# Graph and mixture-of-experts layer: another order of TensorE's work in the mixing part, ranks by a running sum, routing in three steps

## The chip, the cores and the metric

The kernel runs on one core of a Trainium2 chip. The time is the device time of one execution in microseconds (us), the median of three runs. Its engines are TensorE (PE in the profile; PEld are its weight loads), VectorE (DVE), ScalarE (ACT), GpSimd (POOL) and SyncE (SP), which here only issues DMAs.

## What is computed

6250 tokens of 256 numbers, fp32 in and out. Cut to what matters:

```python
xn = layernorm(x)
x = x + graph(xn, src, dst) + mixing(xn)      # mixing: linear attention; it comes down to xn @ M + b
f = layernorm(x)
rh = relu(f @ router_w1 + router_b1)          # 256 -> 128
p = softmax(rh @ router_w2 + router_b2)       # 128 -> 6 experts
top_w, top_i = top_k(p, 2); w = softmax(top_w)
x = x + sum_k w[k] * expert[top_i[k]](f)      # three layers of 256x256, relu after the first two
```

## The kernel before

The program has four stages: tokens are normalised and turned, and the graph's rows are made; keys, values and their products, with the gathers of the graph beside them; the mixing part (some 280 to 440 us of the span); the expert part (to the end). The change is in the third.

**Tokens.** Token `p * 50 + t` stands in partition p (125 of them) and tile t (50). Two tiles are a pair, and the mixing part goes over 25 pairs. Pairs are put together in groups (`SIZES`, six groups of 4, 5, 5, 4, 4, 3 pairs), and routing is done once for each group. A group's rows stand in one of four buffers `xr` until they are scattered.

**One pair.** TensorE makes `x_h @ mix_h + x_h @ mix_l + x_l @ mix_h` and the bias (`mix`, lines 1240 to 1250, 14 products). VectorE adds the token and the graph's sum, and takes mean and variance (`mixed_rows`, L987, L991, L994). ScalarE takes the root (L697); VectorE makes 1/root and -mean/root (`finish2`, L1002, L1004), and the next pair's sum of token and graph (`graph_rows`, L967). ScalarE normalises (L705), TensorE turns the tiles (`turn_rows`, L1259), ScalarE copies them from PSUM (L708), TensorE multiplies by the router's first layer (`hidden`, L1268), ScalarE does the relu (L693), and TensorE the router's second layer (`logits`, L1283; for a group's first pair it starts with the bias, L1279).

**The steps.** Each engine's program is a loop over `i` that is written out by hand, in which pair i is mixed while older pairs are at later stations. TensorE's step i: `hidden(i-2)`, `ranks` of a group whose last pair is i-5, `mix(i+1)`, `logits(i-2)`, `turn_rows(i-1)`. ScalarE's step: relu of i-2, root of i, normalising and eviction of i-1, then an exponential of the routing where one is due. Root and exponential need different function tables, and each change of table is an instruction of its own (ACT_TABLE_LOAD). VectorE's step: `mixed_rows(i)`, `finish2(i-1)`, `graph_rows(i+1)`, then parts of the routing.

**The routing of a group** has four parts on VectorE (`route`, lines 1006 to 1053), in four different steps: part 0 (step of last pair + 2) takes the maximum of the logits; part 1 (+3) the softmax and the first choice of expert; part 2 (+4) the second choice; part 3 (+5) the weights, and the row number of every token in the table of its expert. The one-hot choices are `oh`. The row numbers come from `ranks` on TensorE: one product with a triangle `tri` for the partitions above, one with `base`, the rows already given away, and one more for every tile but the last, which counts it into all later ones. They stand between the second choice and part 3. After part 3 GpSimd scatters the group's tiles into the table `tab0` in DRAM, one indirect DMA for each tile (L566), 50 in all.

**The end of the part.** When all groups are through, one product gives the experts' row ends (L1314), and VectorE makes the tables for the expert part on one partition: how many tiles of 128 rows each expert has (a comparison of 16 x 49 numbers, L1085, L1086), their running sum (L1088, L1090), and for each of 54 tiles and both choices the first row and the expert (L1093 to L1105). SyncE writes six blocks of rows that are to be skipped behind the experts' rows (L453), waits for the tables and all scatters, and loads the first tiles (L469). TensorE, ScalarE and VectorE wait for `tab_done` of both choices before the expert part.

Of the kernel before, what the change touches and what calls it, by code (L numbers as in the profile page):

```python
# [20 lines left out]
P = 125  # L21
# [13 lines left out]
SIZES = (4, 5, 5, 4, 4, 3)  # L35
# [22 lines left out]
AL_STEPS, R_STEPS = 6, 20  # L58
ROUTE_STEPS = (0, 1, 9, 14)
# [3 lines left out]
POOL_C = 14  # L63
# [10 lines left out]
def gps_layer(nc, x, src, dst, w_kv, w_q, w_oT, b_out, w_g, a_l, a_r, rw1, rb1, rw2, rb2,  # L74
              ew1, eb1, ew2, eb2, ew3, eb3, out):
    ctx = ExitStack()
    with ctx:
# [103 lines left out]
        oh = sb("oh", [P, Q, 2, EP], FP32R)  # L181
        rk = sb("rk", [P, Q, 2, EP])
        tw = sb("tw", [P, 8, Q])
        posf = sb("posf", [P, Q, 2])
        pos0 = sb("pos0", [P, RB, Q], I32)
        base = sb("base", [P, 2, EP])
        bsum = sb("bsum", [P, 2, EP])
# [3 lines left out]
        NM = -(-N // S)  # L191
        cnt = sb("cnt", [1, 2, EP])
        nmul = sb("nmul", [1, NM])
        ntl = sb("ntl", [1, 2, EP])
        ge_at = 2 * EP * NM
        gn_at = ge_at + 2 * NTT * E
        tf_at = gn_at + 2 * NTT * E
        ncmp = gsum_sb[0:1, 0:ge_at].rearrange("p (k e m) -> p k e m", k=2, e=EP)
        ends = sb("ends", [1, 2, EP])
        jj = sb("jj", [1, NTT])  # L200
        ge = gsum_sb[0:1, ge_at:gn_at].rearrange("p (k j e) -> p k j e", k=2, j=NTT)
        gn = gsum_sb[0:1, gn_at:tf_at].rearrange("p (k j e) -> p k j e", k=2, j=NTT)
        tf = gsum_sb[0:1, tf_at:tf_at + 16 * NTT].rearrange("p (s k j) -> p s k j", s=8, k=2)
# [44 lines left out]
        rk_ps = d_ps[0:P, 0:Q * 2 * EP].rearrange("p (g k e) -> p g k e", g=Q, k=2)  # L248
# [39 lines left out]
        cnt_done, tstep, tab_done, fill_out = sem("cnt_done"), sem("tstep"), sem("tab_done"), [sem(f"fill_out{k}") for k in range(2)]  # L288
# [196 lines left out]
        def _(pool):  # L485
# [47 lines left out]
            for t in range(T):  # L533
                m, b = t // CH, t // CH % 2
                if t % CH == 0 and m >= 2:
# [14 lines left out]
                      allow_small_or_imprecise_dtypes=True).then_inc(pool_c, 1)  # L550
            pool.iota(desc[:, :], pattern=[[-1, EP]], base=EP, channel_multiplier=0,
                      allow_small_or_imprecise_dtypes=True).then_inc(pool_c, 1)
            pool.iota(tok_all[:, :], pattern=[[1, T]], base=0, channel_multiplier=T).then_inc(pool_c, 1)
            pool.iota(nmul[:, :], pattern=[[S, NM]], base=0, channel_multiplier=0,
# [50 lines left out]
        def _(act):  # L605
# [83 lines left out]

            def step(i):  # L690
                if 0 <= i - 2 < PR:
                    act.wait_ge(rh_done, i - 1)
                    act.activation(rhT[:, :], rh_ps[:, 0:2 * P], ACT.Relu, bias=rb1_sb[:, 0:1]).then_inc(rhT_done, 1)  # L693
                if i < PR:
                    part = slice(i % 2 * 2, i % 2 * 2 + 2)
                    act.wait_ge(ag2_done, 2 * i + 2)
                    act.activation(sd[:, part], mv[:, part, 1], ACT.Sqrt, bias=eps_sb[0:P, 0:1]).then_inc(sd2_done, 1)  # L697
# [22 lines left out]
            for i in range(PR + 6):  # L720
                step(i)
# [678 lines left out]
```

## Time and profile before

| what | us |
| --- | --- |
| median of 3 runs | 796.24 (793.36 to 800.51) |
| the profiled execution's own time | 797.89 |
| its span | 795.7 |
| busy: PE, DVE, ACT, POOL | 676.3, 559.5, 443.0, 402.5 |
| mean granted clock of TensorE | 0.944 of 2.4 GHz |

The span is the time from the first to the last instruction of the profile; the execution's own time has 2.2 us around it. Busy time counts each engine's own instructions; a wait is the idle time before one. In rows of the timeline the columns are start, duration, engine, line, operation, written and read tiles, shape, how many, and in brackets the idle time before it with what ended it. One name can cover several uses: in the mixing part `kv_ps` holds the mixed rows, the hidden layer and some logits, `pt` the turned tiles, `staged` the normalised and the turned rows.

### The profile page before, as it was taken

Reading aid. Unit: us, or ns where it says so; the run is one execution under the profiler, and the core shown is the slowest. Engines: PE = TensorE matmul, PEld = TensorE weight load, DVE = VectorE, ACT = ScalarE, POOL = GpSimd, SP = SyncE. Lnnn points to the kernel's source line nnn. Section 1 sums busy time; section 2 is a strip of 40 time slices with the busy share of each in tenths; the row PEclk is TensorE's granted clock in tenths of the full one; section 3 lists DMA queues with packets and bytes.
Section 4 is the critical chain, followed back from the end, with each engine's and each line's share of the span. In section 5 each row is a group of like instructions: output and inputs, shape, how many; then the busy total and the mean of one; then the engine's idle time right before and its main releaser. Section 6 shows DMA issues by size and latency. Waiting matters only on the chain.

```text
span 795.7 us, 15452 instructions
## 1 busy us (share of the span) xinstructions
PE 676.3 (85%) x4744; PEld 622.7 (78%) x4744; DVE 559.5 (70%) x1399; ACT 443.0 (56%) x874; POOL 402.5 (51%) x443
## 2 busy tenths in 40 slices
PE   3878999999999888888850799999994899999992
PEld 2767788888888777777640699999994799999992
DVE  5674679888888757777645477777773477777772
ACT  2545566767777436677630555656651566565640
POOL 3455378876666000454536155555555155465553
PEclk9999999999999999999955799999998799999997
DMA  8885644444443445765324523443432535444420
GB/s 215 190 157 121 159 125 135 143 127 120 139 125 98 149 145 168 227 187 165 105 59 119 172 89 125 141 137 129 133 115 95 158 92 145 130 134 140 125 74 29
DMA packets 72463, 106.24 MB, mean 134 GB/s; under 512 B 24612, under 2 KB 45605, under 8 KB 72386
## 3 DMA queue, kind: packets, MB, share of 16 engines
q1 hardware_dynamic: 51074, 72.57, 32.4%
q0 software_dynamic: 21312, 32.69, 13.4%
q8 instruction: 43, 0.70, 0.4%
q14 instruction: 34, 0.28, 0.1%
HBM read 60.32 MB, written 46.78 MB: 135 GB/s over the span
## 4 chain that ended last, share of the span: by engine, by line
PE 76%; ACT 6%; DMA 5%; DVE 4%; issue 3%; POOL 3%; SPq 1%; POOLq 0%; DVEq 0%; ACTq 0%
PE kv_ps L1333 10%; PE kv_ps L1335 10%; PE kv_ps L1334 10%; PE pt L1325 6%; PE d_ps L1191 5%; PE kv_ps L1168 5%; PE kv_ps L1171 4%; PE kv_ps L1169 4%; PE kv_ps L1268 3%; PE xt_ps L1325 3%; DMA al_tab<-arena 2%; POOL tab L566 2%; PE pt L1259 2%; ACT staged L708 2%; PE pt L1168 2%
## 5 line engine op out<-in xcount | busy, mean ns | idle before, releaser
L1333 PE MATMUL kv_ps<-we_h,now_h 128*128 x648 | 197.3, 304 | 14.6 <-issue 7.2
L1335 PE MATMUL kv_ps<-we_h,now_l 128*128 x648 | 184.9, 285 | 0.0
L1334 PE MATMUL kv_ps<-we_l,now_h 128*128 x648 | 184.2, 284 | 0.0
L1333 PEld LDWEIGHTS kv_ps<-we_h,now_h 128*128 128x128 f32 x648 | 124.9, 193 | 20.2 <-issue 20.2
L1334 PEld LDWEIGHTS kv_ps<-we_l,now_h 128*128 128x128 f32 x648 | 124.7, 192 | 0.0
L1335 PEld LDWEIGHTS kv_ps<-we_h,now_l 128*128 128x128 f32 x648 | 124.2, 192 | 0.0
L1116 DVE TENSOR_TENSOR work<-kv_ps,be 128x256 f32<-128x256 f32 x216 | 81.7, 419 | 43.1 <-PE kv_ps L1335 43.0
L577 POOL TENSOR_TENSOR arena<-work,arena 128x256 f32<-128x256 f32 x80 | 53.1, 683 | 107.9 <-ACT work L745 107.9
L537 POOL DMA_INDIRECT alg<-al_tab,src_all x50 | 62.3, 1245 | 39.2 <-issue 24.9
L924 DVE TENSOR_REDUCE ss<-xring 125x16 f32<-125x1040 f32 x50 | 61.7, 1234 | 17.4 <-ACT xring L648 16.5
L760 ACT ACTIVATE now_h<-xt_ps 128x512 fp32r<-128x512 f32 x54 | 32.3, 599 | 69.3 <-PE xt_ps L1325 69.3
L540 POOL DMA_INDIRECT arena<-xt_tab,dst_all x50 | 61.8, 1236 | 15.2 <-issue 15.2
L1325 PE MATMUL pt<-ident,staged 128*128 128x128 f32 x216 | 34.2, 283 | 32.0 <-ACT staged L734 32.0
L1135 DVE TENSOR_TENSOR now_l<-pt,now_h 128x512 fp32r<-128x512 f32 x54 | 37.3, 691 | 33.6 <-ACT now_h L752 33.4
L752 ACT ACTIVATE now_h<-pt 128x512 fp32r<-128x512 f32 x54 | 32.3, 599 | 46.0 <-PE pt L1325 46.0
L566 POOL DMA_INDIRECT tab<-work,pos x16 | 19.2, 1199 | 75.7 <-DVE work L1052 71.5
L734 ACT ACTIVATE staged<-arena 128x256 f32<-128x256 f32 x80 | 43.3, 590 | 23.4 <-DMA arena<-tab 23.4
L1191 PEld LDWEIGHTS d_ps<-work 125*128 125x128 f32 x400 | 52.1, 191 | 4.9 <-DVE work L938 0.9
L1191 PE MATMUL d_ps<-work 125*128 125x128 f32 x400 | 52.5, 275 | 0.7 <-DVE work L938 0.7
L1325 PEld LDWEIGHTS pt<-ident,staged 128*128 128x128 f32 x216 | 26.2, 145 | 32.3 <-issue 21.2
L1168 PE MATMUL kv_ps<-wkv_h,x_h 128*128 128x512 f32 x120 | 49.8, 415 | 0.6 <-ACT arena L622 0.6
L1169 PE MATMUL kv_ps<-wkv_l,x_h 128*128 128x512 f32 x120 | 47.1, 392 | 0.0
(239 smaller groups left out, 1823.7 us busy)
## 6 DMA issues: line engine op xcount, KB each, us to landing
arena<-tab SPq DMA_DIRECT2D x40, 259.0 KB, 3.0
xring<-in_x SPq DMA_DIRECT2D x26, 224.0 KB
xt_tab<-arena SPq DMA_DIRECT2D x10, 568.8 KB
arena<-tab SPq DMA_DIRECT2D x40, 131.0 KB, 2.1
we_h<-wt_h SPq DMA_DIRECT2D x6, 768.0 KB, 5.3
we_l<-wt_l SPq DMA_DIRECT2D x6, 768.0 KB, 7.7
weight_in<-tab SPq DMA_DIRECT2D x14, 259.0 KB, 2.9
xring<-in_x SPq DMA_DIRECT2D x5, 560.0 KB
```

The source lines that it names most:

```text
L537: pool.indirect_dma_start(out=alg[:, b, t % CH, :], out_offset=None, in_=al_tab, in_offset=bass.IndirectOffsetOnAxis(ap=src_all[:, t:t + 1 ...
L540: pool.indirect_dma_start(out=xtg[:, b, t % CH, :], out_offset=None, in_=xt_tab, in_offset=bass.IndirectOffsetOnAxis(ap=dst_all[:, t:t + 1 ...
L577: pool.tensor_tensor(row[:, 0:D], b3w[n % 2][:, h, :], row[:, D:2 * D] if k == 0 else row[:, 0:D], ALU.add).then_inc(b3w_done, 1)
L924: dve.reduce_sum(ss[:, t % 2, :], sq[t % 2], axis=AX.X).then_inc(red_done, 1)
L1116: dve.tensor_tensor(rows[:, h, :], outp[:, h, :], be[layer][:, bass.ds(es[j, h] * F, F)], ALU.add).then_inc(finished, 1)
L1168: pe.matmul(outp, x_h[:, t, c, :], w_h(c), start=c == 0, stop=False)
L1169: pe.matmul(outp, x_h[:, t, c, :], w_l(c), start=False, stop=False)
L1191: last = pe.matmul(d_ps[:, at], vs[t % VB][:, at], ks[t % VB][:, at], start=False, stop=t == T - 1, skip_group_check=True)
L1325: last = pe.transpose(outp[:, h, c, :], rows[:, h, c * 128:(c + 1) * 128], ident[:, :])
L1333: pe.matmul(outp, hi[:, c, :], we_h[:, w], start=c == 0, stop=False)
L1334: pe.matmul(outp, hi[:, c, :], we_l[:, w], start=False, stop=False)
L1335: last = pe.matmul(outp, lo[:, c, :], we_h[:, w], start=False, stop=c == KC - 1)
```

## The change

Sizes of the groups, steps of the routing:

```diff
-SIZES = (4, 5, 5, 4, 4, 3)
+SIZES = (4, 5, 4, 4, 3, 3, 2)
-AL_STEPS, R_STEPS = 6, 20
-ROUTE_STEPS = (0, 1, 9, 14)
+AL_STEPS, R_STEPS = 6, 21
+ROUTE_STEPS = (0, 1, 9, 15)
```

TensorE's loop and the ranks (in the loop of all engines `PR + 6` becomes `PR + 4`):

```diff
-                pe.matmul(rk_ps[:, 0:m, :, :], tri[:, :], oh[:, 0:m, :, :], start=True, stop=False, skip_group_check=True)
-                pe.matmul(rk_ps[:, 0:m, :, :], ones[:, :].bitcast(FP32), base[:, :, :].unsqueeze(1).to_broadcast([P, m, 2, EP]), start=False, stop=False,
-                          skip_group_check=True)
-                for g in range(m - 1):
-                    last = pe.matmul(rk_ps[:, g + 1:m, :, :], ones[:, :],
...
+                pe.matmul(rk_ps, tri[:, :], cum[:, :, :, m - 1], start=True, stop=False)
+                last = pe.matmul(rk_ps, ones[:, :].bitcast(FP32), base[:, :, :], start=False, stop=True)
...
-            for i in range(PR + 6):
-                if 0 <= i - 2 < PR:
-                    hidden(i - 2)
-                if i - 5 in ROUTE:
-                    ranks(ROUTE[i - 5])
+            for i in range(PR + 4):
+                if i - 4 in ROUTE:
+                    ranks(ROUTE[i - 4])
                 if i + 1 < PR:
                     mix(i + 1)
                 if 0 <= i - 2 < PR:
-                    logits(i - 2)
+                    hidden(i - 2)
                 if 0 <= i - 1 < PR:
                     turn_rows(i - 1)
+                if 0 <= i - 2 < PR:
+                    logits(i - 2)
```

VectorE's routing: the choices stand as (choice, expert, tile), a running sum over the tiles, `cum`, is made from them, and parts 1 and 2 stand in one step. `carry` holds 0 at each first tile and 1 elsewhere, so that the sum starts anew for each expert.

```diff
-                    choose(1, lg2).then_inc(oh_ready, 1)
+                    link(choose(1, lg2))
                     dve.tensor_tensor(tws[4], tws[3], tws[2], ALU.subtract).then_inc(d_ready, 1)
+                    dve.tensor_tensor_scan(cum[:, :, :, :].rearrange("p k e g -> p (k e g)"), carry[:, :, :].rearrange("p a g -> p (a g)"),
+                                           oh[:, :, :, :].rearrange("p k e g -> p (k e g)"), 0.0, ALU.mult, ALU.add).then_inc(oh_ready, 1)
...
-                    link(dve.reduce_sum(bsum[:, :, :], oh[:, 0:m, :, :].bitcast(FP32).rearrange("p g k e -> p k e g"), axis=AX.X))
                     dve.wait_ge(rk_done, b + 1)
-                    link(dve.tensor_tensor(rk[:, 0:m, :, :], rk_ps[:, 0:m, :, :], oh[:, 0:m, :, :].bitcast(FP32), ALU.mult))
+                    link(dve.scalar_tensor_tensor(rk[:, :, :, 0:m], got, -1.0, bc(rk_ps, m), ALU.add, ALU.add))
+                    link(dve.tensor_tensor(rk[:, :, :, 0:m], rk[:, :, :, 0:m], oh[:, :, :, 0:m], ALU.mult))
...
-                for part in reversed(range(4)):
-                    if i - 2 - part in ROUTE:
-                        route(ROUTE[i - 2 - part], part)
+                for part, lag in ((3, 4), (1, 3), (2, 3), (0, 2)):
+                    if i - lag in ROUTE:
+                        route(ROUTE[i - lag], part)
```

ScalarE's step is put in the order root of i, normalising of i-1, relu of i-2, eviction of i-1; its second exponential comes at the last pair + 3 instead of + 4.

The tables: the number of tiles is found by rounding `cnt / 128` upwards (adding and taking away 2^23), the running sums take three steps over padded copies, and rows and experts take 6 instructions for each choice instead of 12, with a semaphore of its own (`e_done`) for the experts' table:

```diff
-            tlink(dve.tensor_tensor(nc_v, bc(ce, NM), nmul[:, :].unsqueeze(1).to_broadcast([1, 2 * EP, NM]), ALU.is_gt))
-            tlink(dve.reduce_sum(ntl[:, :, :].rearrange("p k e -> p (k e)"), nc_v, axis=AX.X))
...
+            tlink(dve.tensor_scalar(nrm[:, 0, :, :], cnt[:, :, :], 1.0 / S, (S - 1) / (2.0 * S), ALU.mult, ALU.add))
+            tlink(dve.tensor_scalar(nrm[:, 1, :, :], nrm[:, 0, :, :], float(1 << 23), None, ALU.add))
+            tlink(dve.tensor_scalar(ntl, nrm[:, 1, :, :], -float(1 << 23), None, ALU.add))
...
+                dve.tensor_scalar(tab_row[:, k, :], tf[:, 1, k, :], float(E * REG), None, ALU.min).then_inc(tab_done, 1)
+                tlink(dve.reduce_sum(tf[:, 2, k, :], ge[:, k, :, :], axis=AX.X))
+                dve.tensor_scalar(tab_e[:, k, :], tf[:, 2, k, :], float(E - 1), None, ALU.min).then_inc(e_done, 1)
```

Each of TensorE, ScalarE and VectorE now waits for `e_done` of the choice that it starts (`wait_ge(e_done, k + 1)`) instead of for both tables. GpSimd fills `oh` and `carry` in three small instructions more, ahead of the mixing part.

TensorE's program in the step in which the ranks of the first group come, before. `xt_ps` and `kv_ps<-rw_sb` are logits, `kv_ps<-staged` the hidden layer, `pt` the turned tiles, `d_ps` the ranks:

```order
L1283 MATMUL kv_ps<-rw_sb,rhT 125x8 x2
L1259 MATMUL pt<-ident,staged 128x125 x4
L1268 MATMUL kv_ps<-staged,rw_sb 128x250 x2
L1290 MATMUL d_ps<-oh,tri 125x128
L1291 MATMUL d_ps<-base,ones 125x128
L1294 MATMUL d_ps<-oh,ones 125x112
L1294 MATMUL d_ps<-oh,ones 125x96
L1294 MATMUL d_ps<-oh,ones 125x80
L1294 MATMUL d_ps<-oh,ones 125x64
L1294 MATMUL d_ps<-oh,ones 125x48
L1294 MATMUL d_ps<-oh,ones 125x32
L1294 MATMUL d_ps<-oh,ones 125x16
```

The same place now, with the first product of the mixing that follows:

```order
L1289 MATMUL kv_ps<-staged,rw_sb 128x250 x2
L1280 MATMUL pt<-ident,staged 128x125 x4
L1300 MATMUL kv_ps<-rb_sb,ones 125x80
L1304 MATMUL kv_ps<-rw_sb,rhT 125x8 x2
L1311 MATMUL d_ps<-cum,tri 125x16
L1312 MATMUL d_ps<-base,ones 125x16
L1265 MATMUL kv_ps<-bo_hl,sel_hl 128x256
```

Nine products for the ranks have become two. They stood between a hidden layer and a mixing, and now stand at the head of a step, behind the logits; the hidden layer has moved from ahead of the mixing to behind it, and the logits from behind the mixing to the end of the step.

VectorE's program from the second choice of the first group to its rank, before (`y` is token and graph's sum, `arena` the rows):

```order
L1023 TENSOR_TENSOR lg<-lg,desc 125x64
L1024 TENSOR_REDUCE tw<-lg 125x8
L1025 TENSOR_TENSOR oh<-lg,tw 125x8x8
L987 TENSOR_TENSOR arena<-kv_ps,y_1_52 125x2x256
L991 BN_STATS st<-arena 125x6 x2
L994 BN_AGGR mv<-st 125x2 x2
L1002 RECIPROCAL arena<-sd 125x2
L1004 SCALAR_TENSOR_TENSOR arena<-mv,arena 125x2
L967 TENSOR_TENSOR y_0_51<-xring,gsum_sb 125x256 x2
L1039 SCALAR_TENSOR_TENSOR lg<-oh,lg 125x64
L1021 TENSOR_REDUCE tw<-lg 125x8
```

The same place now:

```order
L1048 TENSOR_REDUCE tw<-lg 125x8
L1049 TENSOR_TENSOR oh<-lg,tw 125x8x8
L1063 SCALAR_TENSOR_TENSOR lg<-oh,lg 125x64
L1045 TENSOR_REDUCE tw<-lg 125x8
L1046 TENSOR_TENSOR lg<-lg,tw 125x64
L1047 TENSOR_TENSOR lg<-lg,desc 125x64
L1048 TENSOR_REDUCE tw<-lg 125x8
L1049 TENSOR_TENSOR oh<-lg,tw 125x8x8
L1065 TENSOR_TENSOR tw<-tw 125x8
L1066 SCALAR_TENSOR_TENSOR cum<-carry,oh 125x160
L1011 TENSOR_TENSOR arena<-kv_ps,y_1_52 125x2x256
```

A pair's six instructions stood between the two choices; now they stand behind both and behind the running sum (the 125x160 row).

## Rows read from the trace of the kernel before

**Rows 1.** Page, parts 1 and 2: TensorE's busy time, its granted clock in 40 slices.
```profile
PE 676.3 (85%) x4744; PEld 622.7 (78%) x4744; DVE 559.5 (70%) x1399; ACT 443.0 (56%) x874; POOL 402.5 (51%) x443
...
PEclk9999999999999999999955799999998799999997
```

**Rows 2.** Windows: length, busy time of each engine, clock, DMA share, GB/s.
```profile
343.79:367.87 24.08, 20.21 (x147) 18.08 (x146) 18.34 (x75) 16.77 (x33) 11.93 (x10) 1.00 0.76 240
...
432.60:439.57 6.97, 0.00 (x0) 0.00 (x0) 0.00 (x0) 0.00 (x1) 0.00 (x0) 0.50 0.26 68
```

**Rows 3.** Timeline, ScalarE, one plain step: start us, us, engine, line, what, idle before.
```profile
299.08 0.47 ACT L693 ACTIVATE rhT<-kv_ps,rb_sb 128x250 f32<-128x250 f32 x1 [1.20 <-PE kv_ps L1268]
...
299.64 1.08 ACT L705 ACTIVATE staged<-work 125x256 f32<-125x256 f32 x2
...
301.55 0.59 ACT L708 ACTIVATE staged<-pt 128x500 f32<-128x500 f32 x1 [0.84 <-PE pt L1259]
...
303.35 0.47 ACT L693 ACTIVATE rhT<-kv_ps,rb_sb 128x250 f32<-128x250 f32 x1 [1.20 <-PE kv_ps L1268]
```

**Rows 4.** Timeline, ScalarE: a function table loaded behind pair 5.
```profile
306.43 1.28 ACT L713 ACT_TABLE_LOAD   x1
```

**Rows 5.** Timeline, weight loads of TensorE, one plain step.
```profile
326.23 0.72 PEld L1268 LDWEIGHTS kv_ps<-staged,rw_sb 128*128 128x128 f32 x4 [0.92 <-ACT staged L708]
...
326.97 0.19 PEld L1244 LDWEIGHTS kv_ps<-bo_hl,sel_hl 128*128 128x128 f32 x1
...
328.72 0.52 PEld L1283 LDWEIGHTS kv_ps<-rw_sb,rhT 128*125 128x125 f32 x4
...
329.08 0.50 PEld L1259 LDWEIGHTS pt<-ident,staged 125*128 125x128 f32 x4
```

**Rows 6.** Timeline, VectorE: pair 6 and the four routing parts of group 0.
```profile
305.34 0.22 DVE L1029 TENSOR_REDUCE tw<-xt_ps 125x8 f32<-125x64 f32 x1 [1.91 <-PE xt_ps L1283]
...
305.81 0.68 DVE L987 TENSOR_TENSOR arena<-kv_ps,y 125x512 f32<-125x512 f32 x1
...
308.34 0.21 DVE L1034 TENSOR_REDUCE tw<-lg 125x8 f32<-125x64 f32 x1
...
310.37 0.69 DVE L987 TENSOR_TENSOR arena<-kv_ps,y 125x512 f32<-125x512 f32 x1
...
312.90 0.22 DVE L1039 SCALAR_TENSOR_TENSOR lg<-oh,lg 125x64 f32<-125x64 f32 x1
...
314.33 0.16 DVE L1041 TENSOR_TENSOR tw<-tw 125x8 f32<-125x8 f32 x1
...
317.87 0.17 DVE L1044 TENSOR_SCALAR tw<-tw 125x8 f32<-125x8 f32 x1 [0.27 <-ACT tw L718]
...
319.61 0.17 DVE L1053 TENSOR_TENSOR base<-base,bsum 125x16 f32<-125x16 f32 x1
...
342.92 0.32 DVE L1049 TENSOR_TENSOR rk<-d_ps,oh 125x160 f32<-125x160 f32 x1
```

**Rows 7.** Windows and ScalarE's timeline where TensorE's clock was down.
```profile
380.00:382.00 2.00, 1.99 (x5) 1.67 (x6) 1.83 (x9) 0.00 (x0) 1.39 (x3) 0.50 0.31 91
...
400.00:402.00 2.00, 1.32 (x4) 0.79 (x4) 0.91 (x5) 0.63 (x2) 0.99 (x1) 0.53 0.49 143
...
382.08 0.47 ACT L693 ACTIVATE rhT<-kv_ps,rb_sb 128x250 f32<-128x250 f32 x1 [2.12 <-PE kv_ps L1268]
```

**Rows 8.** Timeline, DMA view and chain of waits, last two groups to expert stage.
```profile
411.89 1.18 POOL L566 DMA_INDIRECT tab<-work,pos  x1 [10.91 <-DVE work L1052]
...
418.51 0.53 DVE L1052 CAST arena<-posf 125x6 int32<-125x6 f32 x1
...
421.34 3.39 SPq L453 DMA_DIRECT2D tab<-skip_rows  x6
...
tab<-skip_rows SPq DMA_DIRECT2D x6, 131.0 KB, 3.4
...
431.41 3.90 DMA tab<-arena,pos
```

More of the change, by code:

```diff
@@ L688, in _, with relu, stdev2 @@
                 act.activation(mix_h[:, c, :], m_ps[c], ACT.Copy).then_inc(mh_done, 1)
+            def relu(i):
+                act.wait_ge(rh_done, i + 1)
+                act.activation(rhT[:, :], rh_ps[:, 0:2 * P], ACT.Relu, bias=rb1_sb[:, 0:1]).then_inc(rhT_done, 1)
+            def stdev2(i):
+                part = slice(i % 2 * 2, i % 2 * 2 + 2)
+                act.wait_ge(ag2_done, 2 * i + 2)
+                act.activation(sd[:, part], mv[:, part, 1], ACT.Sqrt, bias=eps_sb[0:P, 0:1]).then_inc(sd2_done, 1)
@@ new lines, in normal2 @@
+            def normal2(i):
+                g, q = group_of(i), i % 2
+                act.wait_ge(fin2_done, 2 * i + 2)
+                if i >= 2:
+                    act.wait_ge(t2_done, i - 1)
+                for h in range(2):
+                    row = xr[g % RB][:, 2 * i + h - tiles_of(g)[0], :]
+                    act.activation(xnr[:, q, h, :], row[:, 0:D], ACT.Identity, bias=row[:, C_NMR:C_NMR + 1],
+                                   scale=row[:, C_R:C_R + 1]).then_inc(xn2_done, 1)
@@ L694, in step @@
[L694 to L697, printed above, removed]
-                if 0 <= i - 1 < PR:
-                    g, q = group_of(i - 1), (i - 1) % 2
-                    act.wait_ge(fin2_done, 2 * i)
-                    if i >= 3:
-                        act.wait_ge(t2_done, i - 2)
-                    for h in range(2):
-                        row = xr[g % RB][:, 2 * (i - 1) + h - tiles_of(g)[0], :]
-                        act.activation(xnr[:, q, h, :], row[:, 0:D], ACT.Identity, bias=row[:, C_NMR:C_NMR + 1],
-                                       scale=row[:, C_R:C_R + 1]).then_inc(xn2_done, 1)
-                    act.wait_ge(t2_done, i)
-                    act.activation(xTr[:, :, :, 0:P], quad(pt[q])[:, :, :, 0:P], ACT.Copy).then_inc(xT2_done, 1)
+                    relu(i - 2)
@@ L1057, in route @@
                     assert n[0] == (b + 1) * R_STEPS, n[0]
-            for i in range(PR + 6):
+            for i in range(PR + 4):
                 if i < PR:
@@ new lines, in _ @@
+            tlink(dve.tensor_scalar(nrm[:, 1, :, :], nrm[:, 0, :, :], float(1 << 23), None, ALU.add))
+            tlink(dve.tensor_scalar(ntl, nrm[:, 1, :, :], -float(1 << 23), None, ALU.add))
+            tlink(dve.tensor_scalar(coef[:, :, :], ntl[:, :, 0:E], -float(S), float(REG), ALU.mult, ALU.add))
+            for level in range(3):
+                to = scan[:, level + 1, :, pad:pad + EP] if level < 2 else ends[:, :, :]
+                back = pad - (1 << level)
+                tlink(dve.tensor_tensor(to, scan[:, level, :, pad:pad + EP], scan[:, level, :, back:back + EP], ALU.add))
@@ L1300, in _ @@
             mix(0)
-            for i in range(PR + 6):
-                if 0 <= i - 2 < PR:
-                    hidden(i - 2)
-                if i - 5 in ROUTE:
-                    ranks(ROUTE[i - 5])
+            for i in range(PR + 4):
+                if i - 4 in ROUTE:
+                    ranks(ROUTE[i - 4])
                 if i + 1 < PR:
```

94 lines of the change are left out of this document (46 added, 48 removed).

## Prediction

> **What bounds the kernel now.** I read the page first: TensorE is busy 85% of the span, and its clock is full except around slices 21 to 23 [rows 1]. There the mixing part ends, and the chain of waits shows what happens: GpSimd's scatters of the last two groups, one behind the other, then a DMA, then the expert part. From the end of the last scatter to the first row normalised for the experts no engine is busy [rows 2]. The expert part behind it is untouched by the change, and starts when the first tiles are there. So the question is when the last scatter lands, which today is at 431.41 + 3.90 = 435.3 us [rows 8].
>
> Next, the timeline of the mixing part. A plain step (no routing exponential) is 4.27 us from relu to relu [rows 3], and ScalarE is busy in only about half of it: it waits 0.84 for the turned tiles and 1.20 for the hidden layer. That is a ring over two engines: relu 0.47, root, normalising 1.08, wait for the transposes, eviction 0.59, wait for the hidden layer. Where an exponential is due, a table load of 1.28 [rows 4] for it, and one back to the root, lie in the ring; partly they hide in its waits. A group of five pairs took 24.08 us [rows 2], 5 x 4.27 = 21.35 and 2.7 more for its two exponentials. VectorE was busy in 18.34 of the 24.08, so it is the engine that comes next.
>
> **The change, part by part.**
>
> *Order of the steps, plain step.* The new orders cut the ring. TensorE now goes hidden layer, transposes, logits, mixing, and ScalarE has normalised the next pair before it does the relu. What is left is TensorE's own round: hidden layer to relu 0.72 + 0.48 (the wait of 1.20 in rows 3), relu 0.47, logits 0.36, mixing 1.75 (326.97 to 328.72) [rows 5], together 3.8 us. Saved: 0.47 for each plain pair, if nothing else is late.
>
> *Routing in three steps.* VectorE's work for a pair is 2.53 us (305.81 to 308.34); part 0 is 0.47 (305.34 to 305.81), part 1 2.03 (308.34 to 310.37), part 2 1.6 (312.90 to 314.33 and 0.16), part 3 1.9 (317.87 to 319.61 and 0.17) [rows 6]. The new part 2 has one more linked step (0.1) and the running sum over 160 elements. No row shows a running sum; the nearest is the product over 160 elements, 0.32 [rows 6]. I bound it by 0.25 and 0.66 (twice that row) and take 0.40, near the row. Part 3 loses a reduction and gains one operation of like size: no change. A group of four pairs then needs 4 x 2.53 + 0.47 + 2.03 + 2.1 + 1.9 = 16.6 us of VectorE. Part 0 waited 1.91 for the logits [rows 6]; now transposes (0.50 [rows 5]) come ahead of the logits, so I take 2.6. Sum 19.2 us for four pairs, against 4 x 4.27 + 2.7 = 19.8 before. A pair more or less changes a group by the plain step. So a group of n pairs costs 4.27n + 2.7 before and 3.8n + 4.0 now.
>
> Over the part: before 25 x 4.27 + 6 x 2.7 = 123.0; now 25 x 3.8 + 7 x 4.0 = 123.0. The faster plain step is given back by a routing step that is 1.3 dearer, and by a seventh group. The loop gains nothing.
>
> *What waits behind what.* Parts 1, 2 and the sum now stand in one step, 4.5 us of VectorE, and TensorE's ranks stand at the head of the next step, ahead of the mixing, hidden layer and transposes. TensorE runs into the ranks' wait with its queue behind it. Counting from the logits of a group's last pair: VectorE needs 0.5 + 2.5 + 2.0 + 2.1 = 7.1 us to the sum; TensorE has a mixing, a hidden layer, transposes and logits to do, which it has done at about 4.8. It idles some 2.3 us at the ranks, after another wait for the normalising, which is behind two table loads: between 2.5 and 7.1 us it does only four transposes and a few logits. The group time above has that already.
>
> *The clock.* Before, the granted clock was at 1.2 GHz from 380 and again from 400 [rows 7], each time after a stretch in which TensorE waited for an exponential's table loads. A fall makes the wait for the hidden layer 2.12 instead of 1.20 [rows 7, 3]. The new idle stretch, once a group, is longer than those, so I expect a fall at most groups: five in the loop where before had one. Price: 0.9 for the hidden layer, mixing partly covered; 1.0 each, bounds 0 (no falls) and 2.0 (it hits mixing and hidden layer in full). Together +4.0. The Trainium skill, page "TensorE: Matmul & The Clock Gate", section "Why this matters for your kernels", says to leave no idle gaps between bursts of matmuls, since the clock then falls: it speaks against this change, in the direction in which rows 7 point.
>
> On the same footing, "DVE: opcode table, instruction layouts, handler registers and perf-mode slots", section "Datapath and trigger behaviour", says that the built-in running sum goes at half throughput. By that it would cost an estimated 0.47 instead of 0.40, and the sum below would be 0.5 worse over seven groups; no row here shows it.
>
> *Ranks.* Two products of 16 columns for nine or more. In the loop the saving is in the idle time. In the tail it counts: before, the fifth group's ranks and its part 3 stood ahead of the last logits and the last group's part 0. Part 3 alone is 1.9 [rows 6], the ranks some 2 at the low clock, and the third part of the routing comes a step earlier. I take 4.0 for the tail, bounds 2 and 6.
>
> *When the last group is ready.* Before at 418.51 + 0.53 = 419.04 [rows 8]. Now: loop 0, clock +4.0, tail -4.0, first group's ranks and the smaller last group -0.6 (two pairs of chain instead of three: shorter operations). 418.4.
>
> *Scatters.* One takes 1.49 us, issue to issue: 14 ran from 411.89 to the start of the last at 431.41, 19.5 / 13 = 1.50 [rows 8]. Before, the last group's six queued behind the eight of the group before. Now group 5 (six tiles) is ready some 8.5 us ahead of the last and takes 9.0, and the last has four: 418.4 + 0.3 + 0.4 + 3 x 1.5 = 423.6 starts the last one, which lands 3.9 later, at 427.5. Against 435.3 that is 7.8 us less, and this is nearly all of the gain. What is late next: the skipped blocks. They were issued 2.3 us after the last group was ready, over 3.4 us, and land in 3.4 [rows 8]: at 418.4 + 2.3 + 3.1 + 3.4 = 427.2, equal to the scatters. A still smaller last group would gain nothing.
>
> *Tables.* Before, they ran beside the scatters; the new ones need about 4.5 us from the counts, ready at some 423.6, four us ahead of the scatters' landing. Worth 0 in both. If that cover were gone, a slower table would show one for one.
>
> Sum: the profiled execution's 797.89 (its span 795.7 and 2.2 around it) - 7.8 = 790.1; it stood 1.65 above the median 796.24, so the forecast is 796.24 - 7.8 = 788.4.
>
> **Rivals.**
> 1. *The clock holds.* The gaps hold transposes, and before most of the exponentials' steps passed without a fall (the window of a whole group in rows 2 has the full clock). Then the +4.0 is gone: gain 7.8 + 4.0 = 11.8, 784.4. The skipped blocks move with the last group, so they don't cap it.
> 2. *Lost in full.* Each fall costs 2.0, the running sum 0.66, the tail gains only 2: 5 x 1.0 + 7 x 0.26 + 2.0 = 8.8 on top of the sum. Not all of that can be on the path, since VectorE and TensorE are late in turn and what delays one is cover for the other; if half of it is, 7.8 - 4.4 = 3.4 is left: 792.8.
> 3. *Slower: the clock does not come back.* From 400 on it stayed low for the rest of the part, and in slice 23 [rows 1, 7], although TensorE worked. If the rank stall pulls it down and the steps with their gaps never lift it, TensorE's round in a pair is mixing 3.0, hidden layer 1.3, transposes and logits 1.8, some 6.1 us instead of the 4.8 a pair averages (19.2 / 4): +1.3 a pair. From about 6 such pairs (7.8 / 1.3) the gain is gone; with the 18 pairs behind the first group, +23 less the 4 already counted: 796.2 - 7.8 + 19 = 807. Against: behind 380 it came back within some 3 us, as soon as mixing ran in one piece, which it does in each step.
>
> **How the numbers follow.** About 1% is what a measurement of this kernel tells from no change: 788.4 lies on that limit (788.3). Forecast 0.5 (785.5 to 791), clock holds 0.2, lost in full 0.23, slower 0.07. Faster by over 1%: half of the forecast's, all of the first rival: 0.25 + 0.20 and a little of the rest, 0.48. Within 1%: the other half of the forecast's and most of the second rival, 0.46. Slower 0.06. The range goes from 781.5 (first rival with a lucky tail) to 795 (second rival's worse end).
>
> **What would show it.** Right: the mixing part's steps between routing at 3.7 to 3.9 us; a group of four in 19 to 20 us; TensorE idle at the ranks' first product 2 us a group, waiting for the 160-element row; five to seven dips of the clock between 300 and 400; the last part 3 near 418; only four scatters behind it; first tile of the experts normalised near 431.5 instead of 439.57. Wrong: a plain step still at 4.3 (another ring bounds it); the last part 3 before 415 or after 422; the wait for the first tiles ended by the skipped blocks or the tables; an expert part that changes its length, which I take as fixed, though rows now stand in another order in the tables.

## The result, and the profile after

| | before | after |
| --- | --- | --- |
| median of 12 runs each, same chip | 796.39 (793.15 to 801.07) | 791.61 (788.43 to 793.98) |
| ratio | | 0.9932 [0.991, 0.9954] |
| the profiled execution's own time; span | 797.89; 795.7 | 791.61; 789.1 |

The kernel is faster by 0.68%, some 5.4 us, which lies within the 1% that the prediction took as the bound of a change that can be told from none. The forecast was 7.8 us (788.4, range 781.5 to 795). Direction and rough size agree, but the experiments below show that this is partly luck: the shorter row of scatters, to which it gave nearly all of the gain, is there, but the new sizes aren't what makes it; and two large effects of opposite sign stood in it as one sum of zero.

The page of the kernel after, TensorE's busy time and its granted clock, to be held against [rows 1]:

```profile
PE 678.2 (86%) x4705; PEld 622.6 (79%) x4705; DVE 561.4 (71%) x1423; ACT 447.3 (57%) x878; POOL 403.5 (51%) x446
...
PEclk9999999999999999988865899999998899999997
```

Before, slices 21 to 23 showed 5 5 7; now the dips begin earlier and are spread (8 8 8 6 5 8). Where the time went is read from three marks in each trace (us from the start of the first mixed pair, its addition on VectorE; "ready" is the start of the last instruction of the last group's part 3):

| | starts at | last group ready | first expert tile | between these two |
| --- | --- | --- | --- | --- |
| before | 280.63 | 137.95 | 158.94 | 20.99 |
| after | 278.33 | 139.52 | 154.31 | 14.79 |

So of the 6.6 us by which the spans differ, 2.3 lie ahead of the mixing part, in code that is the same but for three small instructions of GpSimd; over all traces of this study that start moves between 275.7 and 280.6. The mixing part gives 4.6: it gets 1.6 longer up to the last group's routing, and 6.2 shorter behind it. The expert part keeps its length (356.1 and 356.5 from the first tile to the end).

*The plain step* came out as worked out. ScalarE's timeline after, one plain step from relu to relu:

```profile
296.13 0.47 ACT L698 ACTIVATE rhT<-kv_ps,rb_sb 128x250 f32<-128x250 f32 x1 [1.48 <-PE kv_ps L1289]
296.56 0.59 ACT L720 ACTIVATE staged<-pt 128x500 f32<-128x500 f32 x1
297.09 0.30 ACT L704 ACTIVATE sd<-mv,eps_sb 125x2 f32<-125x2 f32 x1
297.34 1.09 ACT L714 ACTIVATE staged<-arena 125x256 f32<-125x256 f32 x2
299.89 0.47 ACT L698 ACTIVATE rhT<-kv_ps,rb_sb 128x250 f32<-128x250 f32 x1 [1.46 <-PE kv_ps L1289]
```

299.89 - 296.13 = 3.76 us, where [rows 3] had 4.27. The wait for the turned tiles is gone; ScalarE is idle once a step, for the hidden layer.

*The routing* is where the step's gain is lost. VectorE's timeline from the first group's part 0 (its wait for the logits is 3.08, taken as 2.6) to the running sum, and part 3 behind it:

```profile
301.06 0.22 DVE L1053 TENSOR_REDUCE tw<-xt_ps 125x8 f32<-125x64 f32 x1 [3.08 <-PE xt_ps L1304]
...
304.06 0.21 DVE L1058 TENSOR_REDUCE tw<-lg 125x8 f32<-125x64 f32 x1
...
307.85 0.48 DVE L1066 TENSOR_TENSOR_SCAN cum<-carry,oh 125x160 fp32r<-125x160 f32 x1
308.25 0.67 DVE L1011 TENSOR_TENSOR arena<-kv_ps,y 125x512 f32<-125x512 f32 x1
...
312.50 0.18 DVE L1080 TENSOR_TENSOR base<-base,cum 125x16 f32<-125x16 f32 x1
```

Parts 1, 2 and the sum take 304.06 to 308.25, 4.2 us, in which no pair is served. TensorE stands at the ranks meanwhile, and then mixes at the low clock. Its timeline:

```profile
308.39 0.28 PE L1311 MATMUL d_ps<-cum,tri 125*125 125x16 f32 x1 [1.93 <-DVE cum L1066]
308.52 0.45 PE L1312 MATMUL d_ps<-base,ones 125*125 125x16 f32 x2
308.81 0.56 PE L1265 MATMUL kv_ps<-bo_hl,sel_hl 128*128 128x256 f32 x1
309.17 0.42 PE L1268 MATMUL kv_ps<-wg_h,x_h 128*128 128x256 f32 x1
```

A mixing product is 0.41 us there, and 0.28 where the clock is full. Windows of 2 us around the second group's ranks (columns as in [rows 2]) show the order of events: the busy time falls first, while the clock is still 1.00, and the clock falls behind it. Between 300 and 396 us TensorE was never idle for more than 2.27 at a stretch.

```profile
328.00:330.00 2.00, 0.97 (x5) 0.39 (x3) 1.86 (x10) 1.99 (x5) 0.00 (x0) 1.00 1.02 364
330.00:332.00 2.00, 1.35 (x9) 1.00 (x8) 1.76 (x8) 1.82 (x3) 0.00 (x0) 1.00 0.76 270
332.00:334.00 2.00, 0.37 (x2) 0.37 (x2) 1.86 (x7) 1.16 (x3) 0.00 (x0) 0.64 0.07 27
334.00:336.00 2.00, 2.00 (x11) 2.00 (x11) 1.93 (x9) 1.52 (x4) 0.00 (x0) 0.50 0.00 0
```

The waits of the whole part (280 to 440) have the ranks' seven times, 15.0 us in all. The kernel before had only the last group's, 4.5 us:

```profile
PE d_ps L1311 <- DVE cum L1066: 15.0, 7, 4.6
...
PE d_ps L1290 <- DVE oh L1025: 4.5, 1, 4.5
```

*The tail.* The chain of waits after, from the last group's part 3 on:

```profile
417.70 0.41 DVE pos L1078
...
422.06 0.83 SPq L455
...
423.95 4.49 DMA tab<-skip_rows
...
430.45 2.08 DMA arena<-tab
432.64 1.10 ACT staged L757 x2
```

What ends last is now the skipped blocks, not a scatter (the last of those starts at 423.21). The prediction had the two equal, and the first tile at 431.5. It had also named "the wait for the first tiles ended by the skipped blocks" among the signs of being wrong; with 0.3 us between the two in its own sum (427.2 and 427.5), this sign tells little.

### The profile page after: what moved, and what is told of

Read it like the earlier page. It is cut to its first block, busy times and chain, and to the rows that moved or that the text cites. A ratio compares the mean times of both kernels' runs of the same rounds, so it can differ in the third digit from the quotient of the medians.

```text
span 789.1 us, 15402 instructions
## 1 busy us (share of the span) xinstructions
PE 678.2 (86%) x4705; PEld 622.6 (79%) x4705; DVE 561.4 (71%) x1423; ACT 447.3 (57%) x878; POOL 403.5 (51%) x446
## 4 chain that ended last, share of the span: by engine, by line
PE 74%; DVE 10%; DMA 5%; issue 4%; ACT 3%; SPq 1%; POOL 1%; POOLq 0%; DVEq 0%; ACTq 0%
PE kv_ps L1348 10%; PE kv_ps L1350 10%; PE kv_ps L1349 10%; PE pt L1340 6%; PE d_ps L1212 5%; PE kv_ps L1189 5%; PE kv_ps L1192 4%; PE kv_ps L1190 4%; PE xt_ps L1340 3%; PE kv_ps L1289 2%; DMA al_tab<-arena 2%; PE pt L1189 2%; PE pt L1192 2%; PE pt L1190 2%; PE kv_ps L1270 1%
## 5 line engine op out<-in xcount | busy, mean ns | idle before, releaser
L1340 PE MATMUL pt<-ident,staged 128*128 128x128 f32 x216 | 34.2, 283 | 26.1 <-ACT staged L757 26.1
L571 POOL DMA_INDIRECT tab<-work,pos x14 | 16.7, 1195 | 62.2 <-DVE work L1079 58.6
L1340 PEld LDWEIGHTS pt<-ident,staged 128*128 128x128 f32 x216 | 26.2, 145 | 26.4 <-issue 26.4
```

The costliest lines, as they stand in the source:

```text
L1340: last = pe.transpose(outp[:, h, c, :], rows[:, h, c * 128:(c + 1) * 128], ident[:, :])
```

## The experiments

Each was run beside the kernel before on the same chip; ratios are to it. The chips differ by more than some of the effects, so times in us are compared only within a chip: the kernel before took 795.66 beside sizes undone, two queues, filled and ranks late, 796.48 beside old order, four steps, late and filled and old tables, 799.5 beside order alone, sum alone and small last, and 795.93 beside four steps filled. In the table the groups are the times from the end of one group's routing to the end of the next one's, for the second to the fourth group. They have 5, 5 and 4 pairs with the old sizes (before, sizes undone, and the last five rows), and 5, 4 and 4 with the new. "Ready", "tile" and "tail" are as above, from one profiled execution each; the verdicts go by the ratios.

| kernel | ratio [95%] | groups 2 to 4 | ready | tile | tail |
| --- | --- | --- | --- | --- | --- |
| before | 1 | 24.2, 24.1, 21.1 | 137.95 | 158.94 | 20.99 |
| after | 0.9932 [0.991, 0.9954] | 25.4, 21.6, 21.2 | 139.52 | 154.31 | 14.79 |
| sizes undone | 0.9926 [0.99, 0.9952] | 25.9, 25.2, 21.7 | 138.29 | 154.81 | 16.52 |
| two queues | 0.9926 [0.9899, 0.9953] | 26.0, 21.1, 20.7 | 139.07 | 153.68 | 14.61 |
| old tables | 0.9927 [0.9904, 0.9949] | 25.4, 21.6, 21.2 | 140.02 | 155.00 | 14.98 |
| old order | 0.9954 [0.993, 0.9977] | 26.1, 19.9, 20.4 | 138.80 | 155.26 | 16.46 |
| filled | 0.9878 [0.985, 0.9906] | 23.8, 19.6, 19.5 | 133.98 | 149.91 | 15.93 |
| ranks late | 0.9883 [0.9851, 0.9915] | 25.9, 19.5, 19.6 | 135.96 | 152.24 | 16.28 |
| late and filled | 0.9894 [0.9862, 0.9925] | 23.8, 19.6, 20.1 | 133.45 | 150.23 | 16.78 |
| four steps | 0.9834 [0.98, 0.9868] | 22.5, 24.5, 19.1 | 127.16 | 147.39 | 20.23 |
| order alone | 0.9832 [0.9797, 0.9867] | 22.6, 23.8, 19.6 | 129.85 | 149.15 | 19.30 |
| sum alone | 0.9963 [0.9929, 0.9997] | 26.4, 27.1, 21.1 | 145.89 | 166.89 | 21.00 |
| small last | 0.9816 [0.9776, 0.9857] | 24.6, 22.5, 19.2 | 129.82 | 147.66 | 17.84 |
| four steps filled | 0.9791 [0.9763, 0.9819] | 22.5, 22.5, 19.3 | 123.27 | 144.26 | 20.99 |

### Is it the short last group?

The sizes of before in the kernel after:

```diff
-SIZES = (4, 5, 4, 4, 3, 3, 2)
+SIZES = (4, 5, 5, 4, 4, 3)
```

> The changed kernel with the group sizes of before (4, 5, 5, 4, 4, 3). Forecast's reasoning (nearly all the gain is the shorter queue of scatters behind the last group): loses 3 to 5 us, 795 to 797. Rival (six groups save a routing step of some 4 us, and the skipped blocks no longer end last): the last group is ready 2 us earlier and its scatters queue longer, same time within 1 us, 791 to 792.5.

Measured 790.26 (7 runs), 0.9926 against 0.9932: the sizes are worth nothing that could be measured. The tail is 1.7 longer without them, and the loop 1.2 shorter (one routing less). Yet the tail is still 4.5 shorter than before, with the same eight and six scatters. The timeline of GpSimd shows why:

```profile
412.33 1.19 POOL L571 DMA_INDIRECT tab<-work,pos  x1 [0.30 <-issue]
414.42 1.19 POOL L571 DMA_INDIRECT tab<-arena,pos  x1 [0.90 <-DVE arena L1079]
```

The eight are through when the last group is ready; GpSimd even waits 0.90 for it. The last two groups are 12.6 us apart here, and were 7.1 apart before. Before, the last but one group's part 3 stood in one step with the last group's part 0, directly ahead of it. Routing in three steps puts it one step earlier, and VectorE then waits 5.65 for the last group's logits:

```profile
407.28 0.21 DVE L1053 TENSOR_REDUCE tw<-kv_ps 125x6 f32<-125x48 f32 x1 [5.65 <-PE kv_ps L1304]
```

### Does the clock fall at the ranks, and what does it cost?

Products ahead of the ranks' wait, in all groups but the last. Their output is read by nobody:

```diff
+                for _ in range(16 if b < GROUPS - 1 else 0):
+                    pe.matmul(d_ps[:, D:2 * D], sel_hl[:, :], bo_hl[:, :], start=True, stop=True)
                 pe.wait_ge(oh_ready, b + 1)
```

> The changed kernel with 16 products of 256 columns (sel_hl by bo_hl, into unused columns of d_ps) put ahead of TensorE's wait for the running sum, in six of the seven groups; their result is used nowhere. The changed kernel was 791.6 us. Theory A (the clock): each group's idle stretch lets TensorE's clock fall, and a fall costs about 2 us of the group; with the stretch filled the falls go, the groups of four come down from 21.6 to some 19.5 us, and the time to 783 to 787. Theory B (VectorE bounds the group, the falls are cover): nothing changes, 791 to 793, since the products also stand in the ranks' way by up to 0.1.

Measured 786.52 (6 runs), 0.9878. TensorE's timeline at the second group's ranks: 2.15 us of unread products stand where the wait of 2.27 was, and the mixing behind them has 0.28 a product.

```profile
326.94 2.15 PE L1311 MATMUL d_ps<-bo_hl,sel_hl 128*128 128x256 f32 x16
329.30 0.28 PE L1313 MATMUL d_ps<-cum,tri 125*125 125x16 f32 x1 [0.21 <-DVE cum L1066]
...
329.85 0.28 PE L1268 MATMUL kv_ps<-wg_h,x_h 128*128 128x256 f32 x1
```

The mean clock of 280 to 400 is 0.95 instead of 0.89, and groups of four take 19.5, not 21.4. The prediction's 19.2 for such a group is right. The fall costs 1.6 to 2.0 in each of the groups two to four, but nothing that shows in the later ones: over the whole part filling brings "ready" 5.5 earlier and the time 4.3 down by the ratios, about 1 for each of the five falls. The Trainium skill, page "TensorE: Matmul & The Clock Gate", section "Why this matters for your kernels", advises against idle gaps between bursts of matmuls; the trace agrees in direction.

Not every fall is gone. Two are left in the loop, at 367 and at 384, and the unread products take most of the slow stretch upon themselves: they last 3.34 us there, and the mixing behind them has 0.28 a product again.

```profile
366.48 3.34 PE L1311 MATMUL d_ps<-bo_hl,sel_hl 128*128 128x256 f32 x16
...
370.44 0.28 PE L1268 MATMUL kv_ps<-wg_h,x_h 128*128 128x256 f32 x1
```

### Or is it the work that stands behind the wait?

The ranks behind the mixing and the hidden layer of their step:

```diff
-                if i - 4 in ROUTE:
-                    ranks(ROUTE[i - 4])
                 if i + 1 < PR:
                     mix(i + 1)
                 if 0 <= i - 2 < PR:
                     hidden(i - 2)
+                if i - 4 in ROUTE:
+                    ranks(ROUTE[i - 4])
```

> The changed kernel with the ranks put behind mixing and hidden layer of the same step instead of at its head. Theory A: TensorE does 2.5 us of work while it would have waited, so the wait at the ranks is short, but it has the same work to do and will idle a little later; fewer falls, 787 to 791. Theory B: the last group's readiness depends on VectorE's sum alone, 791 to 792.

Measured 787.13 (6 runs), 0.9883, as good as the filling (its interval just touches that of the kernel after), although the mean clock of 280 to 400 is the same 0.89 as after. Groups of four are 19.5 and 19.6. So the loss of some 2 us a group can be got back in either way: by a full clock behind the wait, or by work that needn't wait. Both together, with 8 unread products ahead of the late ranks, and the two queues of the next section:

> Three edits on the changed kernel together: ranks behind mixing and hidden layer, 8 products of 256 columns ahead of the wait for the running sum, three skipped blocks on ScalarE's queue. Each alone gave 787.1, 786.5 (with 16 products) and 790.3. If ranks late and filling mend the same loss (the clock's), the sum is no more than the better of the two and the queue: 785 to 787. If they add up: 781 to 784.

Measured 788.05 (6 runs), 0.9894: they don't add, as if both acted on one stretch (with 8 products here, not 16). That VectorE's own 4.2 us are what is left of it is argued from the groups, which stay at 19.6 to 20.1, and not shown by itself.

### What ends the tail?

Three of the six skipped blocks of the first choice are issued by ScalarE:

```diff
-                for reg in end_regs:
+                for reg in end_regs[0:3] if k == 0 else end_regs:
...
+            for reg in act_ends:
+                end = act.snap(reg, min_val=0, max_val=(E - 1) * REG + N)
+                act.dma_start(tab0[bass.ds(end, S), :], skip_rows[:, ROW1 - ROW:ROW1]).then_inc(fill_out[0], 16)
```

> The changed kernel with three of the first choice's six skipped blocks issued by ScalarE instead of SyncE. If the skipped blocks are what the first tiles wait for (last landing at 428.4 in the trace of the changed kernel, scatters' landing about 427.1), the first tile comes 1.0 to 1.3 us earlier and the scatters end the wait: 790.5. If they land together by accident, or the landing time grows with the load on the DMA engines, no change: 791.6.

Measured 790.33 (7 runs), 0.9926, not to be told from 0.9932. The chain of waits shows that the releaser did change:

```profile
421.35 4.75 DMA tab<-weight_in,pos
```

The scatter, landing in 4.75, takes over at once: the two were within 0.6 us of each other (tile 153.68 against 154.31), as the prediction had them.

The tables of before, in the kernel after:

```diff
+            tlink(dve.tensor_tensor(nc_v, bc(ce, NM), nmul[:, :].unsqueeze(1).to_broadcast([1, 2 * EP, NM]), ALU.is_gt))
+            tlink(dve.reduce_sum(ntl[:, :, :].rearrange("p k e -> p (k e)"), nc_v, axis=AX.X))
...
```

> The changed kernel with the tables' 31 instructions of before in place of the 20 new ones (semaphores for each choice kept). Forecast's step: the tables of the first choice are done some 2 us ahead of the first tiles' last wait even so, so nothing changes: 791 to 792.5. Rival: the experts' table of the second choice, or the register loads behind them, come after the first tiles: 793 or more.

Measured 790.98 (12 runs), 0.9927. The new tables are worth 0, in their cover, as worked out.

### Which part of the change gives, and which takes?

The kernel after with the orders of before on TensorE and ScalarE:

```diff
+                if 0 <= i - 2 < PR:
+                    hidden(i - 2)
                 if i - 4 in ROUTE:
                     ranks(ROUTE[i - 4])
                 if i + 1 < PR:
                     mix(i + 1)
                 if 0 <= i - 2 < PR:
-                    hidden(i - 2)
+                    logits(i - 2)
                 if 0 <= i - 1 < PR:
                     turn_rows(i - 1)
-                if 0 <= i - 2 < PR:
-                    logits(i - 2)
```

> The changed kernel with TensorE's and ScalarE's step order of before (hidden layer, ranks, mixing, logits, transposes; relu, root, normalising, eviction), and the rest kept: three-step routing, running sum, seven groups, tables. If the new order is what gains (it cuts the plain step from 4.27 to 3.76 us and gives more of VectorE's work cover), this is as slow as before or slower: 794 to 797, plain steps at 4.27. If the order gains nothing in sum, as my forecast had it (it is given back by the routing steps), the gain stays: 790 to 792.

Measured 793.38 (12 runs), 0.9954: in the kernel after, the new order is worth only some 1.8 us, and the two intervals overlap. With the old order, in which the ranks stand behind the hidden layer, TensorE doesn't wait at them in any group but the last. The kernel after with routing in four steps, as before, and the sizes of before:

```diff
-                for part, lag in ((3, 4), (1, 3), (2, 3), (0, 2)):
+                for part, lag in ((3, 5), (2, 4), (1, 3), (0, 2)):
...
-                if i - 4 in ROUTE:
-                    ranks(ROUTE[i - 4])
+                if i - 5 in ROUTE:
+                    ranks(ROUTE[i - 5])
```

> The changed kernel with routing spread over four steps as before (second choice and running sum one step after the first choice, rank one more later) and, since groups of two pairs don't allow that, the sizes of before; to be set beside the run with only the sizes undone, 790.3. If the block of 4.3 us of VectorE work in one step is what makes the idle stretch and the clock falls, the groups come down to 24 us for five pairs and 20 for four from 25 and 21.5, and the time by 3 us or more, less 3 us for the later last group: 788 to 791. If not, 792 to 794 (the later last group alone).

Measured 783.60 (6 runs), 0.9834. Against the kernel with sizes undone only the steps differ, 0.9926 to 0.9834: putting two parts into one step costs 7.3 us by the ratios. That is far more than was expected (788 to 791, beside 790.3). TensorE's timeline at the first group's ranks:

```profile
310.77 0.27 PE L1311 MATMUL d_ps<-cum,tri 125*125 125x16 f32 x1 [0.71 <-DVE cum L1066]
```

0.71 instead of 1.93, and in 300 to 400 us all such waits are 1.4 us, where the kernel after has 9.4. Ready is 11.1 earlier (127.16 to 138.29); the tail gives 3.7 of it back, since the last two groups are again 7.8 apart and their 14 scatters run in one row.

The other way round, the kernel before with only the new orders of TensorE and ScalarE:

```diff
-                if 0 <= i - 2 < PR:
-                    hidden(i - 2)
                 if i - 5 in ROUTE:
                     ranks(ROUTE[i - 5])
                 if i + 1 < PR:
                     mix(i + 1)
                 if 0 <= i - 2 < PR:
-                    logits(i - 2)
+                    hidden(i - 2)
                 if 0 <= i - 1 < PR:
                     turn_rows(i - 1)
+                if 0 <= i - 2 < PR:
+                    logits(i - 2)
```

> The kernel before with the new order of TensorE's and ScalarE's steps alone; ranks with all their products, four routing steps, sizes and tables as before. With running sum and tables added it was 783.6. Theory C (the order gains 0.5 us in each plain pair and the merged routing step took most of it back): 784 to 786, nearly all the 13 us. Rival (order and cheap ranks need each other, since the ranks' 8 to 10 products now stand at the head of the step): 788 to 791.

Measured 785.98 (6 runs), 0.9832: the same as with the running sum, two products and new tables on top. And these alone, with the old order, four steps and old sizes:

> The kernel before with running sum, two-product ranks and new tables, but the order of steps, the four routing steps and the sizes of before. The running sum costs VectorE 0.5 a group and saves one reduction's time, the ranks save TensorE 0.7 to 0.9 a group at full clock. Theory C: the ring of 4.27 hides both, 0 to 2 us less, only in the tail: 794.5 to 796.5. Rival (cheap ranks are what e5 owed its time to): 790 or less.

Measured 797.21 (12 runs), 0.9963 [0.9929, 0.9997]: 0.4%, hardly beyond nothing. With the old order, then, no cost of the merged step is to be seen: the kernel with three steps and seven groups (old order, 0.9954) is no slower than this one with four steps and six groups. The cost shows only with the new order, in which the ranks' wait stands at the head of the step. Its profiled execution, 802.86, was longer than ten of the other eleven, so its row of the table isn't read further. The change is then two things: an order worth 13 us with routing in four steps, and a merged routing step that takes back some seven of these, with the rest around nothing. Filling or late ranks gave some four of the seven back; for the other three VectorE's block of 4.2 us is the candidate, and that isn't shown.

### Can the two remedies be joined?

Four steps with groups of 5, 5, 5, 4, 3, 3 pairs and two queues, for a shorter row of scatters at the end:

> New order, running sum and tables, four routing steps, and sizes (5, 5, 5, 4, 3, 3), with three skipped blocks on ScalarE's queue. In the run with four steps and the sizes of before (783.6) the last group was ready 20.2 us before the first tile, eight and six scatters one behind the other. With six and six the queue is 3.0 us shorter if the group before the last is ready early enough: 780.5 to 782. If that group then ends as late as it did, so that its scatters start as late: 783 to 784.

Measured 786.64 (6 runs), 0.9816: the tail is 2.4 shorter and the loop 2.7 longer, and the ratio cannot be told from 0.9834. A version of the next kernel with such products in the ranks' step as well has no measured time. Four steps with 8 unread products ahead of the transposes, in the step in which TensorE waits for the normalising behind an exponential's table load:

```diff
+                if i - 3 in ROUTE and i < PR:
+                    for _ in range(8):
+                        pe.matmul(d_ps[:, D:2 * D], sel_hl[:, :], bo_hl[:, :], start=True, stop=True)
                 if 0 <= i - 1 < PR:
                     turn_rows(i - 1)
```

> The four-step version (ratio to before 0.9834) with 8 products of 256 columns, used nowhere, ahead of the transposes in the step behind a group's softmax exponential, where TensorE waits 1.1 us for the normalised rows. In that version the clock fell behind this wait in both groups of five and again near 391. Theory A (each fall costs 1 to 2 us): ratio 0.979 to 0.981. Rival (with the merged step gone the falls lie under VectorE's work, or come elsewhere): 0.983 to 0.985.

Measured 779.6 (6 runs, 778.29 to 780.96), 0.9791 [0.9763, 0.9819], the fastest kernel of this study: by the ratios some 11 us below the kernel after and 16.6 below before. Page, the clock in slices:

```profile
PEclk9999999999999999999965999999997899999997
```

Of the dips in the slices only 21 and 22, the end of the part, are left. The slices hide a short one: in windows of 1 us the clock fell at 329, 353 and 391 without the unread products, and with them still at 355 and 393. So one fall of the two in the groups of five is gone, and the group with the other takes 22.5 all the same. Groups of five take 22.5 and 22.5, of four 19.3, that is 3.8n + 3.5 to 4.1. In the tail the last 14 scatters run each directly behind the one before, from 394.00 on, so GpSimd is the bound there. The chain of waits, two of its links before the tiles are loaded:

```profile
411.91 1.19 POOL tab L571
413.41 3.93 DMA tab<-arena,pos
```

## Why the prediction was right, and where it was not

- **Plain step 3.8 us.** Right: 3.76.
- **VectorE's work at a routing, and TensorE's idle time at the ranks.** Right: 1.93, 2.27 and 1.71 us in the first groups, forecast 2.3; a group of four takes 19.5 in the filled kernel, forecast 19.2. VectorE's "4.5 us" for parts 1, 2 and the sum is 4.1 by the prediction's own terms (2.03 and 2.1), and 4.2 in the trace. The running sum was taken as 0.40 and is 0.48. The estimate by half throughput from "DVE: opcode table, instruction layouts, handler registers and perf-mode slots", section "Datapath and trigger behaviour", in the Trainium skill was 0.47, and the trace agrees.
- **"Five in the loop at 1.0 each."** The number of falls was right (309, 333, 353, 377 and 394 us), and so is the sum: +4.0 was forecast, and filling brings "ready" 5.5 earlier and the time 4.3 down. The single price was not: groups two to four lose 1.6 to 2.0 each, where "mixing partly covered" failed, and the later ones nothing that shows. Nor is the wait at the ranks all that brings a fall: the third came at 353.0, 0.6 us before that wait began, and the filled kernel's clock fell at 367 without such a wait, with TensorE at its unread products.
- **"The loop gains nothing."** Right as a sum. Counted from the first mixed pair to the last one's addition on VectorE, before took 114.3 us, the kernel after 119.0, and the filled one 113.5: loop and clock together +4.7, forecast +4.0, and without most of the clock's loss -0.8. It misled as a reading, since it made the seventh group and the merged routing step a fact of the whole change. The runs show two effects of opposite sign and five to seven times the size of the sum of 1.6: the order alone brings ready 8.1 earlier, and merging two parts puts it 11.1 later (sum, ranks and tables take 2.7 off, the sizes add 1.2). The 4.0 for a routed group isn't at fault: the fastest kernel, with four steps, has 3.5 to 4.1 as well. What wasn't worked out is the case with four steps, in which the same stretch takes 107.6 us instead of 117.5 with the sizes undone.
- **The tail, "from shorter scatter queue ... nearly all of the gain".** Size about right (20.99 to 14.79; forecast 20.5 to 13.1), and so is the step "now group 5 ... is ready some 8.5 us ahead of the last" (8.75; the last scatter starts at 423.21, forecast 423.6). What it leaves out is that the merged step does most of this without the new sizes: with the old ones the distance is 12.6 us and eight scatters fit. Some 4.5 of the 6.2 are there without the new sizes, 1.7 come with them, and these cost 1.2 in the loop.
- **Ranks, 4.0 in the tail, and 0.6 for the smaller last group.** Seen only together: from the last pair's addition to the last group's "ready" it was 23.7 us and is 20.5, 3.2 less where 4.6 were forecast. Cheaper ranks with old order and old steps are worth 0.4% of the whole time (interval 0.0 to 0.7%).
- **Last group ready at 418.4.** It was at 418.1, but on a part that had begun 2.3 us earlier. Counted from the first mixed pair it is 139.5, where the forecast's 0.6 earlier gives 137.4: 2.2 late.
- **Skipped blocks next in line; tables worth 0; expert part unchanged.** Right for the kernel after. In six of the other traces, though, the expert part takes 357.6 to 358.8 us instead of 355.8 to 356.7; this wasn't looked into.
- **Rivals.** Clock holds: no. Clock doesn't come back: no; up to 400 it was full again some 3 to 7 us behind each fall. Lost in full: its falls at 2.0 each are what three groups show, and its total (792.8) is nearer to 791.6 than the forecast's 788.4 (gains: 3.4 and 7.8, measured 5.4). 791.6 also lies just above the band of 785.5 to 791 to which the forecast's chance was given.

Open: what moves the start of the mixing part by up to 5 us between traces, in code that is nearly the same. That wasn't tried. The traces show less of the order's 13 us (9.8, tile 158.94 to 149.15) than the ratios do, for which it is no reason, since the tile is counted from that start. The profiled execution of the order alone, 788.15, is the second longest of its six, its expert part is 2.7 us longer than before's, and the traced execution of the kernel before, 797.89, is none of those that ran beside it (median 799.5).

## What to carry to other kernels

Ask of each wait what stands behind it in the same queue: an instruction that waits at the head of a step holds back all work of the step, and the same instruction behind that work costs less (0.5% here). Be wary of gathering a slow engine's side work in one step to save a step of latency: where another engine waits for its end at the head of a step, it cost 0.9% here (0.9834 to 0.9926); with the old order, in which that wait had other work ahead of it, it cost nothing that could be seen. When a change has several parts, work out a case for each part alone, not only the whole, since a sum near zero can hide a large gain and a large loss.

## What the runs showed that I had not expected

- Work saved on TensorE was worth nothing here (two products for the ranks instead of nine, with sum and tables, left the new order's 0.9832 at 0.9834), and work added there can pay: 96 unread products made the kernel 0.5% faster (0.9932 to 0.9878), and 40 made the four-step kernel 0.4% faster (0.9834 to 0.9791), there with intervals that overlap a little.
- The clock went from 1.00 to 0.50 in a loop in which TensorE is busy 84% of the time (100.77 of 120 us), behind the stretch shown above (328 to 334), in which it had transposes, logits and waits of 1.03 and 2.27 us.
- The mean clock alone says little of time: the ranks-late kernel has the same 0.89 as after, and is some 4 us faster; the order alone has 0.90, and is 8 us faster by the ratios. Before has 0.97, and is slower than all of them. I take it that the slow stretches of the ranks-late kernel lie beside VectorE's work; only the length of its groups (19.5) shows that they cost nothing.
- Of two DMAs that write the same table, 4.49 us (skipped blocks) and 3.9 to 4.8 (scatters) pass before the next step can begin. Shortening one showed the other at once.
